# One graph network kernel on one core: gathers of 128 rows, one-hots built by ScalarE, half of the row additions on VectorE, and a second mix that leaves GpSimd out

## The reference, cut to what matters

```python
# one head, twice (the first layer)
xl = x @ Wl; xr = x @ Wr; ee = eattr @ We
xj = xl[src]
h = leaky_relu(xj + xr[dst] + ee, 0.2)
logits = h @ att
ex = exp(logits - segment_max(logits, dst, n)[dst])
alpha = ex / segment_sum(ex, dst, n)[dst]
out = segment_sum(xj * alpha[:, None], dst, n)
# eight heads, once (the second layer)
e = leaky_relu(eh[src] + ee + et[dst], 0.2)
ex = exp(e - e_max[dst])
rst = segment_sum(ft[src] * a[:, :, None], dst, N)
# the second mix
q = q - mean(q); k = k - mean(k)
k2 = l2_normalize(k * k / (sum(k * k) + EPS_DIV), axis=-2)
q2 = l2_normalize(q * q / (sum(q * q) + EPS_DIV), axis=-1)
kv = einsum('bnc,bnd->bcd', k2, v)
attn = v + einsum('bnc,bcd->bnd', q2, kv) / sqrt(N)
return attn @ W_out + b_out
```

## Time and profile before

| | us |
|---|---|
| median of 3 runs | 5197.01 |
| lowest and highest | 5194.62, 5203.74 |
| the profiled execution | 5204.3 |
| its span | 5202.5 |

### The profile page before, as it was taken

How to read it: one execution, slowest core, us unless ns; L and a number is a source line. 1 busy time by engine, 2 the same in 40 slices (tenths; PEclk the granted TensorE clock), 3 DMA queues, 4 the chain that set the end, 5 groups by cost and what they waited for, 6 DMA issues and landing times. The chain is left out here.

```text
span 5202.5 us, 73734 instructions
## 1 busy us (share of the span) xinstructions
PE 4340.8 (83%) x21745; PEld 3584.4 (69%) x21746; DVE 2738.6 (53%) x8592; ACT 2171.7 (42%) x6651; POOL 2022.1 (39%) x1623
## 2 busy tenths in 40 slices
PE   9589999999995899988699998749936888878694
PEld 8478879788794777765577776438935666655694
DVE  2263452634523666764366666363355777766324
ACT  2243434434442666652366666122243333333222
POOL 0000000000004888840488885106618888833141
PEclk9789999999997999996899999659965666579697
DMA  5510000000005555530455553472267656620613
GB/s 141 145 52 10 18 10 1 18 10 18 1 21 124 126 126 125 125 88 19 98 125 127 129 125 83 93 219 68 63 146 151 136 135 135 134 67 25 202 36 87
DMA packets 364626, 463.24 MB, mean 89 GB/s; under 512 B 166429, under 2 KB 296743, under 8 KB 363790
## 3 DMA queue, kind: packets, MB, share of 16 engines
q1 hardware_dynamic: 172546, 258.16, 19.5%
q0 software_dynamic: 191744, 200.92, 17.5%
HBM read 396.61 MB, written 60.67 MB: 88 GB/s over the span
## 5 line engine op out<-in xcount | busy, mean ns | idle before, releaser
L656 POOL DMA_INDIRECT msg_rows<-tab_d,msg_cur x1296 | 1649.9, 1273 | 1762.8 <-DVE msg_cur L142 1368.7
L908 PE MATMUL msg_agp<-msg_rows,msg_oh 125*125 125x261 f32 (+2 forms) x2592 | 849.5, 457 | 14.3 <-DVE ga_acc L792 10.7
L908 PEld LDWEIGHTS msg_agp<-msg_rows,msg_oh 125*125 125x125 f32 x2592 | 549.0, 223 | 125.1 <-DVE ga_acc L792 18.2
L862 PE MATMUL msg_zp<-g_xr,msg_oht 127*125 x1728 | 544.3, 396 | 64.5 <-DVE msg_oht L696 64.2
L866 PE MATMUL msg_zp<-msg_rows,c_ident 125*125 125x256 f32 x1728 | 528.9, 387 | 81.9 <-DMA msg_rows<-tab_d,msg_cur 81.5
L701 DVE SCALAR_TENSOR_TENSOR msg_hid<-msg_zp,g_att 125x256 f32<-125x256 f32 x864 | 360.8, 420 | 334.3 <-PE msg_zp L866 329.5
L960 ACT ACTIVATE msg_dist<-c_iota,c_rel 125x125 f32<-125x125 f32 x1296 | 493.3, 387 | 49.7 <-PEq L3077 34.7
L964 ACT ACTIVATE msg_oh<-msg_dist,c_ones 125x125 f32<-125x125 f32 x1296 | 493.5, 387 | 0.0
L950 ACT ACTIVATE msg_ex<-msg_arg 125x16 f32<-125x16 f32 (+1 forms) x81 | 20.0, 247 | 984.9 <-DVE msg_delta L766 984.9
L866 PEld LDWEIGHTS msg_zp<-msg_rows,c_ident 125*125 125x125 f32 x1728 | 323.9, 190 | 153.7 <-DMA msg_rows<-tab_d,msg_cur 103.6
L792 DVE TENSOR_TENSOR gv_acc<-gv_acc,msg_agp 125x261 f32 (+1 forms) x864 | 364.4, 422 | 72.4 <-PE msg_agp L908 64.9
(11 more groups left out here) (552 smaller groups left out, 7221.1 us busy)
## 6 DMA issues: line engine op xcount, KB each, us to landing
msg_oht<-rel_d SPq DMA_DIRECT2D x81, 875.0 KB
msg_rows<-tab_d,msg_cur POOLq DMA_INDIRECT x1296, 3.9
pl_raw<-in_edge_attr SPq DMA_DIRECT2D x25, 448.0 KB
msg_pens<-pen_d SPq DMA_DIRECT2D x270, 31.2 KB
msg_oht<-rel_d SPq DMA_DIRECT2D x81, 101.6 KB
mix_w<-in_L_mix_W SPq DMA_DIRECT2D x8, 1024.0 KB
m0w_wr<-in_L_ffn_w SPq DMA_DIRECT2D x16, 512.0 KB
m0w_w2r<-in_L_ffn_w SPq DMA_DIRECT2D x16, 512.0 KB
```

Source lines behind the costliest of these rows:

```text
L656: nc.gpsimd.indirect_dma_start(out=rows[:, q, k, :], out_offset=None, in_=table, in_offset=bass.IndirectOffsetOnAxis(ap=cur[:, q, k:k + 1] ...
L862: nc.tensor.matmul(z, hots, d_t, start=True, stop=False)
L908: nc.tensor.matmul(agp[:, sum_bank(u, k), 0:AW], oh[:, u % RB, k, :], rows[:, u % RB, k, 0:AW], start=True, stop=True).then_inc(summed.sem, 1)
```

## The change

- `rows`, `cur` and `src_s` get ROWS = 128 partitions. Each gather of the passes takes 128 rows; the last three indices are zero, and nobody reads those rows.
- `node_hots` goes from VectorE to ScalarE, as two instructions of 125x2000 (|x - p|, then relu(1 - that)), at the head of ScalarE's `body(j)` for group j+2. `edge_hots` writes |rel - column| straight into `oh` and applies the relu to a quarter of a group at a time, 125x500; `dist` is gone. It now waits for the sums of three groups back.
- In one-head passes, for every second pair the two products with the identity are left out. VectorE adds the gathered rows instead (`add_rows`, 125x512, PSUM and SBUF into a new SBUF buffer `both`), and `relu` of that pair reads `both`.
- `rescale` multiplies by a broadcast tensor in place of a per-partition scalar.
- The second mix has no GpSimd code. VectorE does `ksum` and `k2sum` in its loop (`sums`); adding the bias and the closed sums to `x2` (`base`) is moved out of the loop, into VectorE's part behind it, two tiles ahead of the additions of results.

The core of the diff:

```diff
-                            nc.gpsimd.indirect_dma_start(out=rows[:, q, k, :], out_offset=None, in_=table,
+                            nc.gpsimd.indirect_dma_start(out=rows_all[:, q, k, :], out_offset=None, in_=table,
...
+                def add_rows(g, u, p):
...
+                    dve.wait_ge(z_ready.sem, z_ready.at(g * PAIRS + p + 1))
+                    z = zp[:, pair_bank(u, p), 0:2 * D].rearrange("p (a f) -> p a f", a=2)
+                    nc.vector.tensor_tensor(both[:, n % 2], z, rows[:, u % RB, 2 * p:2 * p + 2, 0:D], ALU.add).then_inc(z_used.sem, 1)
...
-                        ch(nc.vector.tensor_scalar(a_t, a_t, fac[:, u % RB, 0:1], None, ALU.mult))
+                        ch(nc.vector.tensor_tensor(a_t, a_t, fac[:, u % RB, 0:1].broadcast_to([P, W]), ALU.mult))
...
-                            relu(j + 1, u + 1, k)
+                            if not by_vector(k // 2):
+                                relu(j + 1, u + 1, k)
+                            elif k % 2 == 0:
+                                add_rows(j + 1, u + 1, k // 2)
+                            else:
+                                relu(j + 1, u + 1, k - 1)
+                                relu(j + 1, u + 1, k)
...
-                            node_hots(j + 2, u + 2, i + (u + 2) // RB)
                             take_sources(j + RB, u)
...
-                        last = nc.tensor.matmul(z, c.ident[0:P, 0:P], rows[:, u % RB, k, 0:D], start=False, stop=True)
+                        if not by_vector(k // 2):
+                            last = nc.tensor.matmul(z, c.ident[0:P, 0:P], rows[:, u % RB, k, 0:D], start=False, stop=True)
...
+                    for b in range(5):
+                        if b < 4:
+                            for k in range(b * QS, (b + 1) * QS):
+                                last = nc.scalar.activation(oh[:, u % RB, k, :], c.iota[0:P, 0:P], ACT.Abs, scale=-1.0, bias=c.rel[:, bass.ds(g * G + k, 1)])
+                            last.then_inc(dist_ready.sem, 1)
...
+                        quarter = oh[:, u % RB, (b - 1) * QS:b * QS, :]
+                        last = nc.scalar.activation(quarter, quarter, ACT.Relu, scale=-1.0, bias=c.ones[0:P, 0:1])
...
+                def node_hots(g):
+
+                    act.wait_ge(hots_landed[g % RB].sem, hots_landed[g % RB].at((g // RB + 1) * hots_in))
+                    h = oht[0:P, g % RB]
+                    nc.scalar.activation(h, h, ACT.Abs, scale=-1.0, bias=c.part[0:P, 0:1]).then_inc(far_ready.sem, 1)
+                    act.wait_ge(far_ready.sem, far_ready.at(g + 1))
+                    nc.scalar.activation(h, h, ACT.Relu, scale=-1.0, bias=c.ones[0:P, 0:1]).then_inc(oht_ready.sem, 1)
...
-            @block.gpsimd
-            def _(pool):
-                ch = Chain(pool, pool_order)
...
+                def sums(t):
...
+                    nc.vector.tensor_tensor(ksum[:], ksum[:], kk[:, t % R], ALU.add).then_inc(kk_summed.sem, 1)
+                    nc.vector.tensor_tensor(k2sum[:], k2sum[:], k2[:, t % R], ALU.add).then_inc(k2_summed.sem, 1)
...
+                def base(t):
+
                     row = x2[:, t].rearrange("p (h f) -> p h f", h=HEADS)
...
+                    nc.vector.tensor_tensor(row, row, acc4[:, t, :, 0:DH], ALU.add).then_inc(closed_ready.sem, 1)
+                    dve.wait_ge(closed_ready.sem, closed_ready.at(NT + t + 1))
+                    nc.vector.tensor_tensor(x2[:, t], x2[:, t], shift[:], ALU.add).then_inc(x2_ready.sem, 1)
...
                 for t in range(NT):
+                    if t + 2 < NT:
+                        base(t + 2)
+                    dve.wait_ge(x2_ready.sem, x2_ready.at(t + 1))
                     dve.wait_ge(out_done.sem, out_done.at(t + 1))
                     nc.vector.tensor_tensor(x2[:, t], x2[:, t], bank(t), ALU.add).then_inc(added.sem, 1)
```

111 lines of the change are left out of this document (63 added, 48 removed).

## The result

The changed kernel took 5405.32 us (median of 4 runs, 5382.99 to 5432.49) against 5195.82 us for the kernel before (4 runs, three of them those of the table above): a ratio of 1.0412, with an interval of 1.0353 to 1.0471. The forecast was 4969 us. The profiled execution is 5432.49 us, 228 us over the 5204.3 of before.

The account below looks back on a forecast made before the run. GpSimd's gathers were taken to bound the one-head passes, a chain through VectorE and TensorE the eight-head pass. Savings 181 + 32 + 15 = 228 us from 5204.3 gave 4976, less 7.3 for the median 4969 us; range 4900 to 5130 (0.8).

Parts of the forecast that it names:

- part 2: One-head passes: a group falls from 25.1 and 25.0 us to 21.7 us, saving 181 us.
- part 3: Eight-head pass: taking the 125x2000 instruction out of the chain through VectorE and TensorE saves 32 us.
- slower: the gather costs by the engine that it is dealt to: Rival, all passes: GpSimd fills 16 queues instead of 5; at 1.35 us a gather, 5285 us; chance 0.06.
- The clock left 0.97: Sign of being wrong: TensorE's granted clock, 0.97 of full, leaves that value in the one-head passes.
- The gather, 1.00 us: All passes: a 128-row gather takes 1.00 us, like evenly dealt 108 rows, against 1.214 for 125; range 0.90 to 1.24.
- A one-head group, 21.7 us, 181 us in all: One-head passes: a group takes 21.7 us, near the gathers' 20.9, between bounds 20.9 and 23.1; saves 181 us.
- Collisions: One-head passes: the 0.8 us a group by which VectorE's 125x2000 one-hot locks out gathers goes away.
- Full blocking by two SBUF inputs: One-head passes: eight relus reading `both` delay GpSimd 2.8 us, group 23.7, saving 71 us; 0.3 us was taken instead.
- ScalarE: Passes: its work rises to 17.4 us a group in one-head passes, is not the bound and stays covered by idle time.
- The eight-head pass, 32 us: Eight-head pass: VectorE's chain loses 1.2 us a group over 27 groups, 32 us; bounds 0 and 119.
- As no gather is waited for: Eight-head pass: reason for taking 32 us and not the 119 us that would follow if gathers held the pass.
- The second mix, 15 us: Second mix: a tile falls from 4.06 to 3.4 us over 23 tiles, saving 15 us; bounds 10 and 19.

Follow-up runs that it names:

- the repeat: The changed kernel without an edit, run again in another set on chip F: 4967.92 us, ratio 0.9548.
- the probe: Program without the reference's computation: dense TensorE products, VectorE additions, ScalarE copies beside ten phases of gathers differing in rows and spacing; 1276.79 us on chip D.
- a_rows126: The changed kernel with gathers of 126 rows instead of 128, on chip B: 4982.34 us, ratio 0.9565.
- c_dvehot126: The changed kernel with 126-row gathers and the node one-hots made by VectorE again as one 125x2000 operation, on chip C: 5012.23 us, ratio 0.9621.

## Why the prediction was wrong, and where it was right

Against the result the prediction was wrong, and in the direction too: 5405 us where 4969 was forecast and 5196 stood before. Against the repeat it was right to 1 us. Both are measurements of the same kernel.

**The step that failed** is the one behind the sum of part 2 and part 3, that a pass costs what its busiest engine or chain costs plus the idle time seen today. The sum had no term for VectorE starting long after the product that it needs. The kernel before, with gathers 1.52 us apart, stands at a distance that the probe shows free of it, and its trace shows 0.1 us at most. The hold-up put 185 us on the first pass (807 against 622), 178 on the second and 72 on the third. The rival "slower: the gather costs by the engine that it is dealt to" had the sign and the place, the 128-row gather, but its mechanism fell: the gather became quicker, 0.949 us, and its break-even was 1.27. The chance of 0.05 for slower was one for price alone, and nothing was set aside for what closer gathers do to others.

The clock left 0.97, which the prediction named as a sign that it is wrong. It is a consequence here: TensorE stands first, at 1662.5 us, the granted clock falls at 1665.7, and its products are slow behind that. The repeat does the same products in fewer us and keeps 0.97. The slower products are 62 of the 185 us.

**Term by term, against the repeat:**

*The gather, 1.00 us.* It is 0.946. The choice of the value "by evenly dealt rows" over that by rows was right, and a little shy. The probes give 0.908 us for 64 rows, 0.933 for 112, 0.946 for 128, 0.997 for 108 and for 126, and 1.211 for 125. By the rule of the Trainium skill that the prediction named (DMA: Bandwidth & Descriptors, "Why a DMA increments its semaphore by 16 and not by 1") these are 4, 7, 8, 9, 9 and 25 rows for an engine, and the order of the prices is that order, with 108 and 126 rows alike: the runs agree in the order. They don't agree in the size: from 7 to 8 rows an engine it is 13 ns more, from 8 to 9 51 ns, so the count of engines (16 below that step, 14 and 12 at it) may have a part.

*A one-head group, 21.7 us, 181 us in all.* It is 21.4 and 21.3 (575.9 and 574.5 over 431 distances, times 16); the passes gave 95 and 90 us, 186. The total is right, and the reason for it half so. Gathers alone would now make it 16 x 1.251 = 20.0; the rest is the wait for TensorE's sums, 35.4 us in 41 waits. The first groups of the pass do take 20.1 to 20.7, and from the eighth on most take 21.6. TensorE is busy 544.7 / 27 = 20.2, as forecast. That the bound is then its lockstep with VectorE and not GpSimd is argued from these waits; no run tests it. The forecast leaned on the gathers' sum; the gather was over-priced by 0.9 us a group, and the lockstep under-priced by about as much.

*Collisions.* In the one-head passes the gathers lasted 0.8 us a group longer than 16 times their median before, and last 0.4 longer in the repeat (0.1 in the first pass of a_rows126, 1.2 in that of c_dvehot126), so half or more of the lockout went. Full blocking by two SBUF inputs, 2.8 us a group, did not come there. (By the prediction's own numbers it would have left 73 us of saving, not 71.) But in the eight-head pass the gathers were 1.3 us a group over their median before and are 1.2 in the repeat, without any one-hot on VectorE. The trace of before already showed the other cause, and the prediction read it too small, at 0.5 us:

```profile
4210.91 2.06 POOL L656 DMA_INDIRECT msg_rows<-tab_d,msg_cur  x1 [0.30 <-issue]
...
4210.63 1.25 DVE L773 TENSOR_TENSOR msg_rows<-msg_rows,msg_ex 125x1056 f32<-125x1056 f32 x1
```

This gather starts when the one-hot has been over for 2.2 us. It starts 0.28 us behind the start of a multiplication of two SBUF tensors, and lasts 2.06 us. The repeat has the same, beside four of them back to back:

```profile
3750.99 1.00 POOL L666 DMA_INDIRECT msg_rows<-tab_d,msg_cur  x1 [0.30 <-issue]
3752.29 2.03 POOL L666 DMA_INDIRECT msg_rows<-tab_d,msg_cur  x1 [0.30 <-issue]
...
3749.91 4.76 DVE L799 TENSOR_TENSOR msg_rows<-msg_rows,msg_ex 125x1056 f32<-125x1056 f32 x4 [0.48 <-ACT msg_ex L982]
```

*ScalarE.* Its work rose to 477 us a pass as reckoned, 17.7 us a group against 17.4, and stayed covered. Its waits for VectorE's exponents, seen in the earlier trace rows as 9.07 us, come from 1680 us on to 201.4 us in 22 waits before and 88.2 in 22 in the repeat: smaller, and still in front of it.

*The eight-head pass, 32 us.* It gave 24 (735 to 711), or 35 between first and last gather, but not by the step named. Taking the one-hot off VectorE's chain was worth 2 us (670.9 to 668.6, on two chips), the quicker gather 16 at 126 rows, and 128 rows another 14 (668.6 to 654.7, on two chips). The step failed on a reading: VectorE does not work without a gap between its one-hot and the logits. A combine there waits for TensorE's sum, and in the repeat, with the one-hot gone, the waits at that place are far longer. Before:

```profile
4210.29 0.43 DVE L792 TENSOR_TENSOR ga_acc<-ga_acc,msg_agp 125x264 f32 x1 [0.33 <-PE msg_agp L908]
```

And in the repeat:

```profile
3974.16 0.43 DVE L818 TENSOR_TENSOR ga_acc<-ga_acc,msg_agp 125x264 f32 x1 [2.45 <-PE msg_agp L940]
...
3976.76 0.43 DVE L818 TENSOR_TENSOR ga_acc<-ga_acc,msg_agp 125x264 f32 x1 [1.29 <-PE msg_agp L940]
```

So at that place the chain goes through TensorE, at 0.64 of its clock, and the 1.25 us turned into waiting, all but the 2 us a pass. That was the prediction's lower bound for this term. "As no gather is waited for" was the weak reason for leaving the gathers out: few waits longer than the issue can still hold a pass when its gathers fill 24.3 of 25.6 us. TensorE's wait for the logits, 3.10 us in the earlier trace rows, is still 2.98.

*The second mix, 15 us.* It gave 21 (163.7 to 142.4 us). VectorE's additions of the keys, of their squares and of the closing in the repeat, to be read against the earlier trace rows:

```profile
4476.90 0.68 DVE L1855 TENSOR_TENSOR sq_qk<-sq_pq,sq_bq 125x512 f32<-125x512 f32 x1
...
4478.64 0.41 DVE L1873 TENSOR_SCALAR ga_ee<-sq_sq,sq_rec,sq_qn 125x256 f32<-125x256 f32 x1
4478.97 0.42 DVE L1880 TENSOR_TENSOR sq_ksum<-sq_ksum,ga_ee 125x256 f32<-125x256 f32 x1
4479.30 0.42 DVE L1881 TENSOR_TENSOR sq_k2sum<-sq_k2sum,ga_ee 125x256 f32<-125x256 f32 x1
4479.64 0.42 DVE L1884 TENSOR_TENSOR ga_acc<-ga_acc,sq_zero 125x256 f32<-125x256 f32 x1
4479.97 0.69 DVE L1855 TENSOR_TENSOR sq_qk<-sq_pq,sq_bq 125x512 f32<-125x512 f32 x1
```

From eviction to eviction a tile takes 4479.97 - 4476.90 = 3.07 us, where the forecast was 3.4. The additions last 0.42 as named, but they overlap, and each costs VectorE only the 0.33 us from one start to the next: three of them make 1.0 where the forecast had 1.26. The scaling of the queries gives back 0.25 where 0.2 was estimated (0.58 to 0.33, start to start). The small operations ahead of it are as they were. TensorE's own 3.25 was too long as well, as it keeps up with 3.07. This term holds in the result too, in spite of the hold-up: there are no gathers in the mix.

*The sum.* 186 + 24 + 21 = 231 us in the repeat, with 4 more elsewhere; 228 were forecast. That the median came out to 1 us is partly luck. The terms missed by +5, -8 and +6 us, the second for a reason that was wrong. The profiled executions are 235 us apart and not 228; the 7 us vanish in the medians, because the forecast took the 7.3 us between profile and median of before over to the new kernel, where they are 1.4.
